# Constant products on TensorE in six waits at the end of a perceiver block on one core

## What is computed

```python
x = x + xattn(layernorm(x), ctx, ctx, ...)   # 16 heads of 64, 2048 context rows per batch
x = x + attn(layernorm(x), ...)              # 8 heads of 16: q/k rotated, scores * decay, no softmax,
                                             # group norm, gate silu(x @ W_G), then @ W_O
x = x + ffn(layernorm(x), ...)
# ffn: xn = normalised x; q, k, v = fff(xn) with three trees
#      y = xn + softmax(q k^T / sqrt(128)) v;  result y + fff(y) with a fourth tree
# fff: 8 levels of a binary tree pick one of 256 leaves for each token;
#      leaf: act(x . w1[leaf] + b1[leaf]) . w2[leaf] + b2[leaf], 16 hidden values
```

## Time and profile before

| | |
|---|---|
| median of 3 runs | 686.81 us (684.99 to 687.1) |
| the profiled execution's own time | 685.5 us |
| its span, first to last instruction | 683.3 us |
| PE busy in the span | 610.8 us (89%) |
| DVE, ACT, POOL busy | 451.3, 394.2, 280.1 us |
| mean granted clock of PE | 0.955 |

### The profile page before, as it was taken

How to read it: one execution, slowest core, us unless ns; L and a number is a source line. 1 busy time by engine, 2 the same in 40 slices (tenths; PEclk the granted TensorE clock), 3 DMA queues, 4 the chain that set the end, 5 groups by cost and what they waited for, 6 DMA issues and landing times.

```text
span 683.3 us, 10760 instructions
## 1 busy us (share of the span) xinstructions
PE 610.8 (89%) x4122; PEld 539.5 (79%) x4122; DVE 451.3 (66%) x798; ACT 394.2 (58%) x835; POOL 280.1 (41%) x266
## 2 busy tenths in 40 slices
PE   3789999999999999897999999989999998875664
PEld 2578888898898989786989898778989897744554
DVE  2565656677776777775777777766777776842833
ACT  2465566566655655667655854957556756521541
POOL 3110001120202106896252347886161549944831
PEclk9999999999999999999999999999999999965795
DMA  9610000020100007140030037210210052203812
GB/s 210 189 47 1 1 1 1 1 62 2 62 1 1 1 1 275 44 128 0 1 129 1 1 100 283 75 55 0 84 46 1 5 197 120 66 1 127 337 60 121
DMA packets 21353, 48.52 MB, mean 71 GB/s; under 512 B 1460, under 2 KB 14648, under 8 KB 17208
## 3 DMA queue, kind: packets, MB, share of 16 engines
q0 software_dynamic: 4608, 34.74, 13.6%
q1 hardware_dynamic: 16008, 12.79, 6.9%
q10 hardware_dynamic: 688, 0.33, 0.2%
HBM read 47.59 MB, written 0.26 MB: 70 GB/s over the span
## 4 chain that ended last, share of the span: by engine, by line
PE 64%; POOL 16%; DVE 8%; ACT 6%; DMA 3%; issue 3%; ACTq 0%; POOLq 0%
PE ps_s L421 23%; PE ps_av L421 20%; PE ps_ring L641 13%; POOL leaf L1368 5%; PE ps_m L421 4%; PE ps_ring L421 3%; POOL leaf L1372 3%; ACT prob L942 2%; POOL leaf L1409 2%; DVE chunk_max L1225 2%; DMA leaf<-up_v_dram,idx 2%; ACT pt_hi L879 1%; POOL ct_lo L1337 1%; DVE pt_lo L1027 1%; DMA ident<-ident_in_dram 1%
## 5 line engine op out<-in xcount | busy, mean ns | idle before, releaser
L879 ACT CAST pt_hi<-ps_ring 128x512 fp32r<-128x512 f32 x256 | 144.5, 590 | 150.5 <-PE ps_ring L641 150.2
L1027 DVE TENSOR_TENSOR pt_lo<-ps_ring,pt_hi 128x512 fp32r<-128x512 f32 x256 | 170.3, 686 | 62.8 <-ACT pt_hi L879 62.7
L942 ACT ACTIVATE prob<-ps_s,neg_max 128x1024 f32<-128x1024 f32 x128 | 141.7, 1114 | 34.9 <-DVE neg_max L1308 34.7
L641 PE MATMUL ps_ring<-ident,prob 128*128 128x128 f32 x1024 | 145.7, 275 | 14.1 <-DVE x_sb L1257 4.9
L1225 DVE TENSOR_REDUCE chunk_max<-ps_s 128x1 f32<-128x1024 f32 x128 | 150.7, 1216 | 3.9 <-PE ps_s L421 3.8
L421 PE MATMUL ps_av<-pt_hi,c_hi 128*128 128x256 f32 x512 | 151.3, 296 | 0.0
L641 PEld LDWEIGHTS ps_ring<-ident,prob 128*128 128x128 f32 x1024 | 117.5, 141 | 41.1 <-issue 23.6
L421 PE MATMUL ps_av<-pt_lo,c_hi 128*128 128x256 f32 x512 | 144.7, 283 | 0.0
L421 PE MATMUL ps_av<-pt_hi,c_lo 128*128 128x256 f32 x512 | 144.6, 282 | 0.0
L421 PE MATMUL ps_s<-ct_hi,q_hi 128*128 128x512 f32 x256 | 113.4, 443 | 7.0 <-ACT prob L942 5.4
L421 PE MATMUL ps_s<-ct_hi,q_lo 128*128 128x512 f32 x256 | 102.4, 400 | 0.0
(11 more groups left out here) (256 smaller groups left out, 752.5 us busy)
## 6 DMA issues: line engine op xcount, KB each, us to landing
stage<-ctx_t_dram SPq DMA_DIRECT2D x16, 256.0 KB, 3.1
stage<-ctx_rows_dram SPq DMA_DIRECT2D x16, 256.0 KB, 3.0
leaf<-w_v_dram SPq DMA_DIRECT2D x1, 512.0 KB, 10.8
leaf<-w_o_dram SPq DMA_DIRECT2D x1, 512.0 KB, 12.6
dec<-decay_dram SPq DMA_DIRECT2D x1, 512.0 KB
nw<-node_w_dram SPq DMA_DIRECT2D x1, 510.0 KB
wsm<-w_small_dram SPq DMA_DIRECT2D x1, 448.0 KB
leaf<-wq_t_dram SPq DMA_DIRECT2D x1, 384.0 KB, 8.3
```

Of the source, the lines that this page charges most:

```text
L641: last = nc.tensor.transpose(o[:, i * P:(i + 1) * P], prob[:, n % 2, k:k + P], ident[:])
L879: nc.scalar.copy(pt_hi[:, pp, row:row + KPC, P * (n % 2):P * (n % 2 + 1)], ps_ring[:, i % 2, :].rearrange("p (k q) -> p k q", k=KPC)).then ...
L942: nc.scalar.activation(prob[:, n % 2, 1024 * e:1024 * (e + 1)], ps_s[:, 1024 * e:1024 * (e + 1)], ACT.Exp, bias=neg_max[:, n:n + 1], accum ...
L1027: return nc.vector.tensor_tensor(o, a, b_, op)
```

## The change

PE gets a helper that issues a number of products of `ways` with itself, 128x512 in bfloat16, all into bank 1 of `ps_ring`. Their results are read by nobody. It is called at six places: ahead of the waits of `att` (5 products) and `attv` (8) of batch 2, and of `gated_t` (11) and `xf_t` (12) of batch 3, inside `third_sum` (18) and inside `leaf_sum(3)` (38). Ahead of the first, PE waits for the last reader of `ps_ring`, DVE's last addition of a head's output.

```diff
+WARM = {("att", B - 2): 5, ("attv", B - 2): 8, ("gated_t", B - 1): 11, ("xf_t", B - 1): 12}
+WARM_THIRD, WARM_LAST = 18, 38
...
+            def warm(count):
+
+                for i in range(count):
+                    mm(ps_ring[:, 1, :], ways[:, 0, 0:P], ways[:].rearrange("p c n -> p (c n)"))
+
...
                     pe.wait_ge(S[f"got_down{t}"], 16 * B)
                     add(rows[:, W1:DOWN_ROW], t < 3)
+                    if t == 3:
+                        warm(WARM_LAST)
                     by_act(0, n // 2)
...
                 pe.wait_ge(S["got_down3"], 16 * (B - 1))
                 mm(o, ident[:], rows[:, W1:DOWN_ROW], False, False)
+                warm(WARM_THIRD)
                 pe.wait_ge(S["own_ready"], 1)
...
                 m, tr, xn1 = ps_rest[b], transposed[b], normed[b]
+                if (k, b) == ("att", B - 2):
+                    pe.wait_ge(S["ring_free"], BY_DVE[("X", HEADS + 3, 0)])
+                warm(WARM.get((k, b), 0))
```

## The result

| | before | with the change |
|---|---|---|
| median of 20 runs each | 686.06 us (683.66 to 688.41) | 689.33 us (687.35 to 691.0) |
| ratio with its 95% interval | | 1.0051 [1.0037, 1.0064] |
| profiled execution, own time / span | 685.5 / 683.3 us | 689.98 / 687.8 us |
| mean granted clock of PE | 0.955 | 0.98 |

A forecast was written before the change was run, and what follows sets the result against it. PE at half clock was taken to bound two tail stretches and the final sum. Loss 6.2 us in the last place less gain 3.35 in the first five gave +2.85 on 686.81: 689.7 us, range 686.3 to 692.7.

The forecast's parts named there:

- The last place: 38 products between the last gathered rows' landing and the first block delay the final sum: loss 6.2 us, 5.7 to 6.9.
- The price of a product: Each added bfloat16 product of 512 columns on PE takes 0.43 us at half clock and 0.23 at full.
- rival of cheap products: Products cost less than score products, down to 0.12 us at full clock: net about -0.2, 686.6 us; chance 0.06.
- The first five places: 54 products in PE's waits from `att` to `third_sum` raise the clock for the steps there: gain 3.35 us.
- one fall, near 609: PE's clock falls once, in the 2.0 us left idle ahead of `attv`, and rises at 614.1; chance 0.48.
- the rival in which the clock never falls: PE's clock stays full between 601 and 632: gain 5.55, loss 6.2, so +0.65, 687.5 us; chance 0.24.
- term (a): PE's 8.79 us from `attv` to the end of `yv`, 609.37 to 618.16: gain 3.9 us at full clock.
- Term (b): `gated_t` and `wo` at full clock gain only 0.2 us, as POOL meanwhile issues batch 2's two gathers.
- signs of being wrong: Last products issued before the landing; clock holding 601 to 632 and rising early at the end; or `gated_t` or `xf_t` later.
- moves as a whole: The gather of 10.41 us from 639.15 shifts unchanged with whatever comes ahead, so the earlier gain reaches its issue in full.
- the last fill lies inside the wait: Rows land some 3 us before 672.26, so the 38 products fit the wait and the sum runs faster: 678.3 us; chance 0.05.
- the fills run at half clock: The early products themselves run at half clock and delay `gated_t`: gain only 0.35, so +5.85, 692.7 us; chance 0.17.

The follow-up runs named there:

- e2: The changed kernel with only the 38 products behind the landing of the gathered rows, the other five places empty: 692.67 us, ratio 1.0101 to before.
- e1: The changed kernel without the 38 products in the last place, the first five places kept: 682.76 us, ratio 0.9956 to before.
- e4: The changed kernel without the eight products ahead of `attv`: 692.89 us, ratio 1.009 to before.
- e5: The changed kernel without the five products ahead of `att`: 689.85 us, ratio 1.0059 to before.
- f1: As e11, but with 44 products ahead of the last landing in place of 38, and five behind it: 679.28 us, ratio 0.9927 to before.
- e7: The changed kernel with only the 38 products, moved ahead of the wait for the last gathered rows, other places empty: 685.98 us, ratio 1.0006 to before.
- e3: The changed kernel with its last 38 products moved ahead of the wait for the gathered rows: 682.37 us, ratio 0.9949 to before.
- e6: The changed kernel with 19 products in place of 38 in the last place: 685.45 us, ratio 1.0000 to before.
- e11: As e3, with nine more products ahead of the wait for the rows of `down_q`: 680.77 us, ratio 0.9937 to before.
- e9: As e3, without the 18 products in `third_sum`: 681.43 us, ratio 0.9938 to before.
- e7b: Another profiled execution of the unchanged e7 kernel, which took 688.43 us.
- e7c: A further profiled execution of the unchanged e7 kernel, which took 685.86 us.

## Why the prediction was right, and where its steps were off

The forecast was 689.7 us and the median is 689.33. The mechanism of the loss was right; of the gain, only the sum was, and that by luck.

*The last place* was forecast at +6.2 us (5.7 to 6.9). e2 against before has +6.75, the change against e1 has 3.27 + 3.16 = 6.4, and in the two profiles the time from the landing to the end of the sum goes from 8.73 us (672.26 to 680.99) to 15.15 (670.37 to 685.52), +6.4. The parts: the rise came 5.9 us behind the landing (676.27 by the 0.73 of the window) and not 4.7, so about 12 products ran at half clock and 26 at full, and the sum took 3.73 us against 3.8. With 38 products behind the landing the rise came 3.4 (e4, e5) to 6.0 us (e2) after it, about the 3.6 to 6.1 that the range was made of.

*The price of a product.* In f1, 44 products take 9.66 us and 5 take 1.24: 8.42 / 39 = 0.216 each at full clock, against the 0.23 I took from the score products; at half clock 0.43, as forecast (e4). The row from which I took the half-clock price was a poor witness: at 17.13 the products stand 0.43 us apart, but the window from 17.0 to 18.0 has a granted clock of 1.00, so that no row shows half clock there. The rival of cheap products is out. The Trainium skill, "TensorE: Matmul & The Clock Gate", section "Back-to-back issue gap", gives some 216 ns for an isolated gap and 131 ns in a stream of weight loads and matmuls: the trace agrees with the first, in a stream, and 131 appears in no run here.

*The first five places* were forecast at 3.35 us, and e1 has 3.2. But the step behind the number failed: "I therefore expect one fall, near 609". It took the length of the idle stretch, 2.0 us against 1.60, for what decides. After the eight products the 1.95 us of idle (forecast 2.0) brought none, and A shrank by 5.6 us between the two profiles, which is the 5.55 of the rival in which the clock never falls (term (a): 8.79 us became 5.05 from `attv` to the end of `yv`, a gain of 3.74 against 3.9). Term (b) was small for the reason given: between `wo` and `xf_t` the chain is POOL's two gathers.

Of the signs of being wrong that the prediction named, one came by half: the clock held through the stretch, almost to 632, but did not rise early at the end. Two things that the sum did not have made it come out all the same. First, A of the one profile before was high. Without products in these places five executions have 38.0, 36.2, 35.7, 36.3 and 36.6 us, 36.6 in the mean, since the clock falls and rises at other moments each time (in e7 it was at half from 602.5 to 612.7 and from 619.6 to 629.8, before for all of 602 to 632); with the eight it is 32.4 in seven and 32.6 in e5. The usual gain is 4.2 us. Second, B gives some back, which I had set at nothing when I wrote that all of the gain arrives at the gather's issue and the gather "moves as a whole": 24.4 to 24.8 us without products, 25.1 to 25.5 with them in five executions (the gather of `up_v` takes 11.22 us in the change and 10.41 before; 10.9 to 11.6 in all nine executions with products in the early places, 10.3 to 10.8 in the five without), and 27.2 to 27.3 in e3, e5 and e6, where the clock was at half for 6.8 us from 640 to 642 on (3.4 us in e1, which has 25.5, and 3.3 us from 647.4 on in e4, which has 26.7). -4.2 + 0.7 and C's +6.7, which is from one profile each, make +3.2; measured is +3.3. With the 27.2 it would be 5; the profile of the change shows no such fall, but whether some of its 20 runs had one is not known.

*The fall near 640* was not among my steps. With the early clock the third sum ends sooner than the rows of `down_q` land, PE waits 2.4 to 2.8 us in e1, e3, e5 and e6, the clock falls, and a sum that was hidden before (the chain went through the gather of `up_v`) becomes the path. e11 agrees: nine products in that wait leave 0.46 us of it, the clock holds, and B is back at 25.1. It is not proof by itself, since the change held its clock there in one profile without the nine (1.58 us of wait, B 25.2), and the intervals of e11 and e3 overlap.

*The other rivals.* That the last fill lies inside the wait was wrong, as the row said: the landing is after 9.69 us of idle. That the fills run at half clock is what e4 shows, when the eight are missing. I took 686.81 us for before, and over 20 runs it is 686.06, 0.75 lower; the move was +3.27 and not +2.85, 0.42 more. The two nearly cancel, and leave the forecast 0.4 us off. Two figures of the prediction are off without weight in it: the clock before rose at 632.57 and not 632.53 (0.93 in the half microsecond), and 18 products at half clock would be 2.0 us late and not 1.9.

What stays open is why the gathers of `up_v` and `up_f` take 10.3 to 11.6 and 6.0 to 7.2 us, and what sets the moment of a fall in one execution and not in the next.

## What to carry to other kernels

Work that only keeps PE's clock up belongs ahead of the wait that it is to bridge, and at most a few products behind it: 38 behind the landing cost 6.75 us, 44 ahead and 5 behind it (with the other places) gained 5.2. Fit the count to the wait at full clock: in the four profiles in which the products ended 1.2 to 2.4 us ahead of the landing (e9, e11, e7b, e7c), the clock fell around it. Look also for the wait that an earlier finish opens next. Last, measure a stretch from its own start in several executions before a gain is priced from one: here part A without the eight or any other early product lay between 35.7 and 38.0 us.

## What the runs showed of the hardware that was not expected

The length of an idle stretch alone does not tell whether the granted clock falls. It fell in 1.60 us (before) and in 1.69 (e5), and held through 1.95 (the change, behind eight products) and 1.63 (e9). Two executions of one kernel show it best, at the same product with the same idle stretch, e7_only_ahead and then e7b_look, in the timeline of PE:

```profile
602.72 0.76 PE L425 MATMUL ps_m<-tr_sb 128*128 128x128 f32 x2 [1.70 <-ACT tr_sb L852]
```

```profile
605.92 0.46 PE L425 MATMUL ps_m<-tr_sb 128*128 128x128 f32 x2 [1.70 <-ACT tr_sb L852]
```

In e7 the clock fell at 602.5, in that stretch; in e7b it held until 607.9, and the product took 0.46 us and not 0.76.

The time from the start of PE's work to the rise varies far more than the 3.6 to 6.1 us that the prediction read from before: 3.5 us in e1 (640.52 to 644.06), 5.9 in the change's last place, and 13.0 us in e4 (PE works from 610.59, the clock rises at 623.54), although PE was busy for 12.69 of 13.5 us there. Before has such a stretch too: there the clock stays at half from 601.85 to 632.57, with PE at work in 20.16 of 30.5 us.

The tail begins at a different time in every execution, 600.8 to 604.8 us in 14 profiles with the same program ahead of it. That is almost as wide as the spread between the runs of one kernel (683.66 to 688.41 for before), so that much of this spread may well come from there. e7b and e7c are a case of it: the same kernel, A, B and C together 79.2 and 79.6 us, the tail's start at 604.8 and 601.9, and own times of 688.43 and 685.86. No run was made to show it for the others.
